# A decoder layer: second attention turned end to end with block-wise value rows, its scores in 64-row matmuls

## The reference

```python
x = layernorm(x + attn(x, Wq, Wk, Wv, proj_w, proj_b))     # 16 x 256 tokens, D = 256, 16 heads of 64, causal
x = layernorm(x + xattn(x, ctx, ctx, mask, w_q, w_k, w_v, w_o))
x = layernorm(x + moe(x, ...))                             # 8 experts and a fallback, top 2, with a capacity

def xattn(q, k, v, mask, w_q, w_k, w_v, w_o):              # ctx: 16 x 77 x 256; 16 heads of 16
    Q, K, V = (proj(q, w_q), proj(k, w_k), proj(v, w_v))
    scores = einsum('bhqd,bhkd->bhqk', Q, K) / sqrt(16)
    attn = softmax(where(mask == 0, -1e9, scores))
    return einsum('bhqk,bhkd->bhqd', attn, V) @ w_o.T
```

## Time and profile before

| | |
|---|---|
| median of 3 runs | 1551.44 us |
| the profiled execution: span | 1547.9 us |
| the profiled execution: its own time | not listed apart; 1550.63 to 1551.74 in the runs |
| TensorE (PE) busy | 1359.4 us, 88% |
| VectorE (DVE) busy | 1137.0 us, 73% |
| ScalarE (ACT) busy | 925.7 us, 60% |
| GpSimd (POOL) busy | 729.5 us, 47% |
| TensorE clock granted, mean | 0.959 |

### The profile page before, as it was taken

How to read it: one execution, slowest core, us unless ns; L and a number is a source line. 1 busy time by engine, 2 the same in 40 slices (tenths; PEclk the granted TensorE clock), 3 DMA queues, 4 the chain that set the end, 5 groups by cost and what they waited for, 6 DMA issues and landing times. The chain is left out here.

```text
span 1547.9 us, 49899 instructions
## 1 busy us (share of the span) xinstructions
PE 1359.4 (88%) x17713; PEld 1140.1 (74%) x17713; DVE 1137.0 (73%) x3181; ACT 925.7 (60%) x2255; POOL 729.5 (47%) x923
## 2 busy tenths in 40 slices
PE   3599999999999999999999999864999999999940
PEld 2488888888888888888888887642688888888830
DVE  4678888888888888888888888748555555555538
ACT  3566777777777777777777756514344444444426
POOL 3135555564574575565566543420333334333326
PEclk9899999999999999999999999995999999999975
DMA  9667667667667666757666564019211411111135
GB/s 216 136 149 161 160 175 143 134 168 145 140 147 166 136 136 175 141 130 172 142 145 150 137 104 87 17 67 422 81 50 46 159 45 50 48 50 48 49 124 212
DMA packets 254604, 199.79 MB, mean 129 GB/s; under 512 B 180158, under 2 KB 212030, under 8 KB 251936
## 3 DMA queue, kind: packets, MB, share of 16 engines
q1 hardware_dynamic: 243328, 174.70, 47.2%
q0 software_dynamic: 6816, 17.71, 3.7%
q10 hardware_dynamic: 4224, 4.19, 0.8%
HBM read 93.79 MB, written 65.93 MB: 103 GB/s over the span
## 5 line engine op out<-in xcount | busy, mean ns | idle before, releaser
L1664 PE MATMUL ps_e<-xt,wres 128*128 128x128 f16 x3408 | 354.4, 220 | 0.6 <-issue 0.6
L1664 PEld LDWEIGHTS ps_e<-xt,wres 128*128 x3408 | 287.8, 98 | 72.6 <-issue 0.9
L1720 ACT ACTIVATE act_g<-ps_e,b 128x128 f32<-128x128 f32 x568 | 162.5, 369 | 223.9 <-PE ps_e L1664 115.8
L1671 PE MATMUL ps_e<-wres,g_hi 128*128 x568 | 214.5, 379 | 1.3 <-DVE g_lo L1750 1.3
L724 ACT ACTIVATE probs<-st_k,nmax 128x128 f32<-128x128 f32 (+1 forms) x512 | 199.9, 448 | 2.1 <-DVE nmax L931 2.0
L1623 POOL DMA_INDIRECT z_scr<-e_y,dst_i x71 | 83.5, 1176 | 220.5 <-DVE e_y L1741 220.5
L931 DVE CUSTOM_DVE_ANT_0 st_k<-ps,causal 128x128 f32<-128x128 f32 (+1 forms) x512 | 160.6, 351 | 32.6 <-PE ps L449 32.6
L731 ACT ACTIVATE pt_hi<-ps 128x384 f16<-128x384 f32 x256 | 125.0, 488 | 55.0 <-PE ps L457 31.5
L1673 PE MATMUL ps_e<-wres,g_lo 128*128 x568 | 154.8, 273 | 0.0
L1201 POOL TENSOR_TENSOR o_st<-o_norm,o_st 128x256 f16<-128x256 f32 x128 | 86.3, 674 | 127.2 <-ACT o_st L739 124.6
L936 DVE TENSOR_TENSOR pt_lo<-ps,pt_hi 128x384 f16<-128x384 f32 x256 | 141.3, 552 | 4.4 <-ACT pt_hi L731 1.9
(11 more groups left out here) (273 smaller groups left out, 4316.7 us busy)
## 6 DMA issues: line engine op xcount, KB each, us to landing
k_pair<-k_pair SPq DMA_DIRECT2D x96, 256.0 KB, 6.4
st_p<-in_moe_w SPq DMA_DIRECT2D x24, 768.0 KB, 5.8
w_scr<-st_p SPq DMA_DIRECT2D x24, 768.0 KB, 4.1
wres<-w_scr SPq DMA_DIRECT2D x18, 1024.0 KB, 19.7
v_scr<-v_tok SPq DMA_DIRECT2D x32, 512.0 KB, 3.7
v_pos<-v_scr SPq DMA_DIRECT2D x64, 256.0 KB, 6.2
q_st<-st_q SPq DMA_DIRECT2D x64, 128.0 KB, 3.4
z_scr<-zero SPq DMA_DIRECT2D x32, 256.0 KB, 3.6
```

The source lines that it names most:

```text
L1664: last = mm(out, w(c * FF + f * P, b, P), xt[:, t % 2, a, c], start=(m == 0), stop=(m == 5))
L1671: mm(out[:, 0:2 * D], g_hi[:, t % G_BUFS, f], w(KC * FF + f * D, 0, 2 * D), start=(f == 0), stop=False, skip_group_check=True)
L1720: nc.scalar.activation(act_g[:, k % 2, f], ps[:, 3 + 2 * (k % 2) + f // 4, (f % 4) * P:(f % 4 + 1) * P], ACT.Gelu, bias=bias[:, f:f + 1], ...
```

## The change

1. The probabilities of 8 heads x 77 keys lie in one row of 616 columns, padded to 640. They are transposed in 5 blocks of 128 columns (3 in one bank, 2 in the other), across the borders of heads. The copies behind are 384 and 256 columns on 128 partitions.
2. To match, the values are needed by block: `value_rows` (new, TensorE and ScalarE, once a batch and half) repeats the 77 value rows with a selection matrix `key_rows`, so that row p of block c holds the key that stands in column 128 c + p, for each of the 2 or 3 heads of the block (12 slots, 408 columns with high and low parts); `own_values` (new, GpSimd) multiplies by `slot_heads`, which leaves each slot its own head's rows. `pv2` then has 5 x 3 matmuls of 128 rows and 34 or 51 columns.
3. The scores use 64 rows: bank j needs only rows 64 j to 64 j + 63 of the block-diagonal keys, which are therefore kept 4 heads wide, and the two banks' matmuls alternate. `spread_k2` writes half the columns.
4. `value_constants` (new, GpSimd, before step 1) makes `key_rows` and `slot_heads`.
5. All `sem_inc(s_held...)` instructions are removed, in every phase.

```diff
 # scores (TensorE)
-for j, bank in enumerate(banks2(t, cc)):
-    for m, (a, b) in enumerate(((q2_hi, 0), (q2_lo, 0), (q2_hi, 1))):
-        last = mm(bank[:, 0:4 * CTX], a[:, cc], k2_bd[:, b, cc, 4 * j:4 * j + 4], start=(m == 0), stop=(m == 2))
+for m, (a, b) in enumerate(((q2_hi, 0), (q2_lo, 0), (q2_hi, 1))):
+    for j, bank in enumerate(banks2(t, cc)):
+        rows = slice(j * P // 2, (j + 1) * P // 2)
+        last = mm(bank[:, 0:4 * CTX], a[rows, cc], k2_bd[rows, b, cc], start=(m == 0), stop=(m == 2))
 # turn
-    for n in range(4):
-        last = transpose(bank[0:CTX, n * P:(n + 1) * P], probs2_of(t, cc)[:, 4 * j + n], ident[:])
+    for n, c in enumerate(BANK_CHUNKS[j]):                    # ((0, 1, 2), (3, 4))
+        last = transpose(bank[:, n * P:(n + 1) * P], probs2_of(t, cc)[:, c * P:(c + 1) * P], ident[:])
 # x1's transposes (c6) wait longer
-pe.wait_ge(s_kv2_lo, 2 * (half(t) + 1))
+pe.wait_ge(s_vrow_in, 2 * (half(t) + 1))
 # new on TensorE: value_rows(s-1, 0) behind pv(s, 0), value_rows(s-1, 1) behind turn_probs(s, 1)
+def value_rows(t, cc):                                        # t even only
+    if cc == 0:
+        pe.wait_ge(s_kv2_lo, 2 * (b + 1))
+        if t == 0: pe.wait_ge(s_slots, N_SLOTS)
+    else:
+        pe.wait_ge(s_vrow_in, 2 * b + 1)
+    for c in range(CHUNKS2):
+        last = mm(c6[:, at:at + n * 34], key_rows[:, c * P:(c + 1) * P], v2[:, h:h + n], start=True, stop=True)
+    last.then_inc(s_vrow, 1)
 # pv2
-for n in range(HB): (three matmuls, 17 or 16 columns, high[:, n] or low[:, n] of 77 rows)
+for c in range(CHUNKS2): (three matmuls, n * 17 columns, high[:, c] or low[:, c] of 128 rows, v2_own)
 # new on ScalarE: value_rows(s-1, 0) behind piece(s-4), value_rows(s-1, 1) behind pt(s, 1)
+act.wait_ge(s_vrow, 2 * b + cc + 1)
+activation(v2_rows[:, cc], c6[:, 0:HEAD_SLOTS * 34], ACT.Copy).then_inc(s_vrow_in, 1)
 # new on GpSimd: own_values(s-1, 0) behind shift(s-1, 0), own_values(s-1, 1) behind split_o(s, 1)
+pool.wait_ge(s_vrow_in, 2 * b + cc + 1)
+if b >= 1: pool.wait_ge(s_pv2, 2 * t)
+tensor_tensor(v2_own[:, cc], v2_rows[:, cc], slot_heads broadcast to 34 columns a slot, ALU.mult).then_inc(s_vown, 1)
 # moments, split, predicated, the experts' steps and SyncE's waits, for example
 dve.wait_ge(s_ln, t + 1)
-dve.sem_inc(s_held_dve, 1)
 nc.vector.bn_aggr(mv[:, ln], stats[:, ln]).then_inc(s_mv, 1)
```

More of the change, by code:

```diff
@@ L25 @@
 HB = P // DK
+CHUNKS2 = (HB * CTX + P - 1) // P
+PADDED = CHUNKS2 * P
+FIRST_HEAD = [c * P // CTX for c in range(CHUNKS2)]
+HEADS_IN = [min(HB - 1, (c * P + P - 1) // CTX) - c * P // CTX + 1 for c in range(CHUNKS2)]
+SLOT_AT = [sum(HEADS_IN[:c]) for c in range(CHUNKS2)]
+HEAD_SLOTS = sum(HEADS_IN)
+BANK_CHUNKS = ((0, 1, 2), (3, 4))
 E = 8
@@ L81, in attention_block @@
     causal = sb("causal", [P, 3, P], F32)
-    head_rows = sb("head_rows", [P, HB, CTX], F16)
+    head_rows = sb("head_rows", [P, HB // 2, CTX], F16)
     mask = sb("mask", [P, 2, CTX], I32)
@@ L557, in pv2 @@
                 pe.wait_ge(s_lgc, t)
[L558 to L564, removed]
+            if cc == 0 and even(t):
+                pe.wait_ge(s_vown, 2 * (half(t) + 1))
+            high, low = pt2_of(t, cc)
+            for c in range(CHUNKS2):
+                n, at = HEADS_IN[c], (HB * cc + FIRST_HEAD[c]) * (1 + DK)
+                out = c7[:, at:at + n * (1 + DK)]
+                v_hi, v_lo = (v2_own[:, cc, SLOT_AT[c]:SLOT_AT[c] + n, k] for k in range(2))
+                mm(out, high[:, c], v_hi, start=(c == 0), stop=False, skip_group_check=True)
+                mm(out, high[:, c], v_lo, start=False, stop=False, skip_group_check=True)
+                last = mm(out, low[:, c], v_hi, start=False, stop=(c == CHUNKS2 - 1), skip_group_check=True)
             last.then_inc(s_pv2, 1)
@@ L610, in step @@
                 pv(s, 0)
+            if has(s - 1):
+                value_rows(s - 1, 0)
             if has(s - 2):
@@ L1175, in constants @@
-            pool.wait_ge(s_const, N_CONST)
+            for n, rows in enumerate((slice(0, P // 2), slice(P // 2, P))):
+                pool.wait_ge(s_const, N_CONST - 4 + 2 * n)
+                nc.gpsimd.affine_select(out=head_rows[rows], in_=head_rows[rows], compare_op=ALU.is_ge, fill=0.0, base=0,
+                                        pattern=[[-DK, HB // 2], [0, CTX]], channel_multiplier=1).then_inc(s_const, 1)
+                pool.wait_ge(s_const, N_CONST - 3 + 2 * n)
+                nc.gpsimd.affine_select(out=head_rows[rows], in_=head_rows[rows], compare_op=ALU.is_ge, fill=0.0, base=DK - 1,
+                                        pattern=[[DK, HB // 2], [0, CTX]], channel_multiplier=-1).then_inc(s_const, 1)
@@ L1288, in _ @@
         pool.sem_inc(s_w_lo, 1)
-        run(step, {-1: constants})
+        run(step, {-1: constants, 1: value_constants})
 def weight_rows(io):
@@ L1582, in experts_block @@
     s_w = keep["s_w"]
-    s_held = keep["s_held"]
     xg = keep["xg"]
```

142 lines of the change are left out of this document (88 added, 54 removed).

## The result

The change makes the kernel faster: 1524.03 us, median of four runs (1523.41 to 1524.60), beside 1551.04 for the kernel before in the same session (1550.09 to 1551.74). The ratio is 0.9823, 95% interval 0.981 to 0.9837. The gain of 27.0 us is twice the 13.4 forecast: inside the wide range of 1515 to 1558, outside the forecast's own range of 1527 to 1547.

A forecast was written before the change was run, and what follows sets the result against it. TensorE, though busy nearly all the time, bounds only B to P; chains through GpSimd set the rest. Terms sum to -0.89 us a pair, -13.8 over 15.5 pairs, ends 0: 1538 us, own range 1527 to 1547, wide 1515 to 1558.

The forecast's parts named there:

- six stretches: Odd plus even step, cut at F (first value fill), B (second transposed-probability group), P (turn after output projection); -0.89 us a pair.
- Removed increments: On GpSimd and VectorE, 0.09 to 0.11 us each: -0.38 in each P to F, -0.09 in the context split.
- Own values on POOL: Two multiplications on GpSimd in odd steps, 0.9 us each, against 1.19 idle: +0.6 in odd F to B.
- Transposes: On TensorE, five instead of eight, twice a tile: -0.34 us in each B to P.
- Value rows: Ten TensorE matmuls every second tile, 0.4 us in even B to P; +0.1 counted, the rest covered.
- Even F to B: Stretch set by GpSimd: one cast's increment gone and earlier ScalarE copies, together -0.15 us.
- Scores: Six TensorE matmuls a group, now on 64-row halves: between 0.4 us less and no change, counting nothing.
- Value matmuls: On TensorE, 15 instead of 24, 0.38 us instead of 0.61; counted as nothing.
- Ends: +2 us before step 2 for value constants on GpSimd, -2 us in the last tile; sum 0.
- A: Rival: TensorE is the bound throughout, 1521 us, or 1495 with overlapped score halves; chance 0.13.
- B: Rival: GpSimd eats the saving, an own-value multiplication costing 1.28 us; 1549, no change; chance 0.12.
- C: Rival: 64-row score matmuls alternate without overlap, 1.0 us more a group; 1575, slower; chance 0.13.

The follow-up runs named there:

- e1: The changed kernel with the increments behind waits put back on VectorE and GpSimd alone; 1541.1 us, ratio 0.9926.
- e2: The kernel before with every increment behind a wait removed on all engines and nothing else changed; 1533.86 us, ratio 0.9885.
- e5: The changed kernel with both own-value multiplications moved on GpSimd to directly behind the second key spreading; 1518.42 us, ratio 0.9783.
- e6: The changed kernel with GpSimd's split of x (tile s + 2) moved to the head of its step; 1518.50 us, ratio 0.9784.
- e7: The changed kernel with GpSimd's even-step context split moved behind the second softmax shift and the output split; 1513.26 us, ratio 0.9750.
- e10: The changed kernel with each own-value multiplication done twice, the extra one into a spare tile; 1546.39 us, ratio 0.9964.
- e3: The changed kernel with scores over 128 rows again, keys spread over 8 heads, banks one after the other; 1532.62 us, ratio 0.9874.
- e4: The changed kernel with its 64-row score matmuls ordered bank 0 three times, then bank 1, instead of alternating; 1524.24 us, ratio 0.9822.
- e8: The changed kernel with the moves of e5, e6 and e7 together, plus value constants ahead of the first key spreading; 1506.31 us, ratio 0.9708.

## Why the prediction was half right

*The bound.* Right, and the failure is one of sizes. Of the six stretches the forecast had the sign of five; "B to P is TensorE's own" and "P to F and F to B are chains through POOL" hold in e1, e2, e5, e6, e7 and e10.

*Removed increments* (-0.38 twice, -0.09 in the context split: -0.85 a pair). **First mis-sized term**: e2 measured -1.32. The chain in step 15, as distances behind P15 before and after: statistics 0.89 and 0.66, aggregate 1.47 and 1.12, first split operation 3.23 and 2.74, cast 4.25 and 3.67, F15 7.73 and 7.02. Of the 0.71, 0.12 comes at the aggregate, 0.14 at the first split operation (the idle time before it falls from 0.67 to 0.54, while deviation and norm keep their distances), 0.10 at the first cast and 0.12 behind it, where the second cast stands: four increments at 0.10 to 0.14, where I had 0.11 and three times 0.09 from one gap each.

The first 0.23 is ahead of all these, at the statistics, and it is the turning's: e1, with the increments in, has the statistics at 0.66 as well. The second residual, on which they wait, in before and in e1:

```profile
508.41 0.41 DVE L1029 SCALAR_TENSOR_TENSOR y<-ps,x 128x256 f32<-128x256 f32 x1
```

```profile
506.17 0.42 DVE L1066 SCALAR_TENSOR_TENSOR y<-ps,x 128x256 f32<-128x256 f32 x1 [0.51 <-PE ps L598]
```

It starts 0.45 behind P15 before, behind the norm ahead of it on VectorE, and 0.20 in e1, where it waits for TensorE's output projection; in after it is 0.20 too. In e2 it is 0.34: the first norm's aggregate passes an increment too, which I had left out. So of the 0.47 that my price lacked, 0.26 are in the odd P to F (0.11 of them in step 15 by this increment ahead of P), 0.08 in the even one, and 0.09 in the odd F to B, priced at nothing, where the increment of the masked copy stood ahead of VectorE's maximum, for which the shift waited. The rest is in the even F to B and in rounding.

*Own values on POOL* (+0.6 in odd F to B). **Second mis-sized term**: +0.22, and +0.26 in e1. The shift starts 8.03 behind F15 instead of 7.76, 0.27 later. Counted from start to start, GpSimd of before, beside 512.61 and 513.29 of after:

```profile
521.53 0.73 POOL L1230 TENSOR_TENSOR x_bias<-x_nat,proj_b 128x256 f32<-128x256 f32 x1
```

Two multiplications add 1.65 or 1.66. From x_bias to the shift were 1.92 (521.53 to 523.45), and now are 0.68: 1.24, not the 1.19 that the profile calls idle, because operations on POOL follow each other 0.05 before the profiled end of the one ahead. From the first of the three pieces to the second split_o were 3.50, and now are 3.35 (508.62 to 511.98): 0.15, since POOL no longer waits for ACT there. 1.66 - 1.24 - 0.15 is 0.27. That POOL becomes the bound here was right (e10); I had taken 0.9 for 0.83, the smaller idle time, and nothing for the second wait.

Against the whole miss of 0.84 a pair, 13 us over 15.5 pairs: 0.47 is the increments (e2) and 0.34 the own values (0.6 less the 0.26 of e1). The smaller terms below miss by another 0.2 on the same side, and 0.18 of all this is counted twice. That these last two cancel is luck.

*Transposes.* -0.34 was forecast for each B to P; the odd one gave -0.41 alone and -0.47 with the rest, and the wait for o_st's low part (0.13 before, 0.04 after) is part of that. *Value rows.* 0.4 was forecast on TensorE; twice five matmuls take 0.19 each in step 16, 0.38, and the even B to P shows it in full: +0.02 instead of -0.34. But the next odd P comes later against a norm on VectorE that does not wait for it (its end is 0.53 behind P before, 0.19 after), and the odd P to F is 0.31 shorter in e1. Net -0.29, forecast -0.24: the mechanism and its size were right. *Even F to B* -0.27 (-0.15): increments 0.12, the turning 0.16. The parts don't quite add: 1.32 + 0.59 is 1.91, together 1.73. The 0.18 is in the odd P to F (0.63 and 0.31, together 0.76): the residual of the norm can't start before TensorE's projection, which the turning alone reaches (0.45 to 0.20) and to which the increment ahead of it (0.45 to 0.34) adds nothing.

*Scores.* "Counts nothing", between 0.4 less and no change: 0.2 less a group with the way in and out. For the first half that is hidden behind ACT, as forecast. For the second half it is not: e3 gives back 0.22 in the odd F to B, so without the shorter scores F to B would have grown by about 0.4. *Value matmuls* 0.38: 0.39. *Ends.* +2 at the start was +1.0 (+1.8 in e1 and -1.0 in e2, though P2 scatters by as much), and the tail -2 was -2.3.

*The rivals.* A (TensorE bound) is out by e1 and e2; that its 1521 lies nearest to the result is chance. B (POOL eats it) has the right mechanism, and e10 shows what it takes: the multiplications would have to cost more than twice as much. C is out by the rows of the score pairs. Of the signs named, F15 to B15 grew, so POOL is the bound, but by a third of what was forecast. A wait of about 1 us on ACT before B15 is not there (515.31 has no idle time before it), and before B16 it is 0.70. A wait of TensorE at the value rows, named as a sign against me, is there once, 2.3 at the start.

## What to carry to other kernels

Read the stretches between events that different engines set, and take each engine's gaps in them: here TensorE was 88% busy, and 16 us lay in instructions on GpSimd and VectorE that compute nothing, 0.10 to 0.14 us each on a chain that passes them. Work put on a helper engine cost no more here than its length less the idle time of that one stretch (0.22 to 0.27 of a possible 0.47); placed in another gap (1.90 us ahead of the first shift) it cost next to nothing, and order alone gave 26 us more (1524.03 to 1497.82). Price a small instruction from several rows with and without it, not from one gap.

## What the hardware showed that I had not expected

Matmuls on the two 64-row halves start beside each other even when three of one half stand in the kernel's list ahead of the other's (10 ns apart in e4, 3 in after). The first norm on VectorE (128x256, L977 before, L1008 after) takes 0.40 to 0.41 us in every even step from 6 to 25 of every run, where no key spreading runs beside it. In the odd step 15, beside the spreading, it takes 1.05 before, 0.90 after, 0.75 in e3 and 0.56 in e8. In e1 it takes 0.40, and there the second spreading operation beside it takes 0.86 instead of 0.74. So the one or the other is held up; no run here isolates what decides it.
